# Attention step of a pipelined decoder: TensorE's groups in a new order, with ScalarE and VectorE following

## What is computed

```python
xn = layernorm(x)
q, k, v = xn @ Wq, src @ Wk, src @ Wv          # src is xn, or ctx in a cross attention
s = einsum('bhqd,bhkd->bhqk', q, k) * scale (+ mask or relative positions)
o = softmax(s) @ v
x = x + o @ Wo (+ bo)                          # L1_xattn, L3_xattn: a layer norm after it
```

## Time and profile before

| what | value |
|---|---|
| profiled execution | 4900.09 us, its span 4898.2 us |
| median of three runs | 4896.48 us |
| TensorE busy | 4007.7 us, 82% of the span |
| VectorE, GpSimd busy | 65%, 61% |
| mean granted TensorE clock | 0.889 |
| DMA | mean 28 GB/s |

### The profile page before, as it was taken

One profiled execution on the slowest core, in us unless ns is written; L12 is line 12 of the kernel. 1 busy time (PEld: TensorE's weight loads), 2 busy tenths in 40 slices (PEclk: granted clock), 3 DMA queues, 4 the chain that ended last, 5 costly groups with the idle time before them and its releaser, 6 DMA issues. The chain is left out here.

```text
span 4898.2 us, 215645 instructions
## 1 busy us (share of the span) xinstructions
PE 4007.7 (82%) x85067; PEld 2918.6 (60%) x85076; DVE 3203.4 (65%) x10848; ACT 2059.5 (42%) x5737; POOL 2994.6 (61%) x4949
## 2 busy tenths in 40 slices
PE   8999977254899978656999997559879998889988
PEld 6777754132566666523777774335547776667766
DVE  5875668422344688787556874753337878888866
ACT  4555545011344444365555554112225543336632
POOL 6766632276455699688556762038876777777710
PEclk9999988555899998755999997879998999999999
DMA  3000012433100022200000002113431000000000
GB/s 94 5 13 19 19 28 57 78 62 54 37 0 0 18 39 39 35 1 1 2 0 15 22 18 54 42 46 75 77 62 35 0 15 16 16 9 1 0 13 24
DMA packets 380509, 139.58 MB, mean 28 GB/s; under 512 B 216487, under 2 KB 373239, under 8 KB 380055
## 3 DMA queue, kind: packets, MB, share of 16 engines
q1 hardware_dynamic: 345430, 107.60, 9.3%
q0 software_dynamic: 34816, 28.34, 4.0%
HBM read 91.46 MB, written 43.85 MB: 28 GB/s over the span
## 5 line engine op out<-in xcount | busy, mean ns | idle before, releaser
L1051 DVE TENSOR_REDUCE rowmax<-ps 128x16 f32<-128x1024 f32 x512 | 626.3, 1223 | 488.0 <-PE ps L678 487.7
L696 PE MATMUL ps<-prob,kT 32*64 32x256 f32 x9216 | 781.7, 408 | 8.7 <-issue 2.4
L721 PE MATMUL ps<-v,probT 64*64 64x64 f32 x36864 | 764.6, 227 | 5.3 <-issue 2.2
L721 PEld LDWEIGHTS ps<-v,probT 64*64 64x64 f32 x36864 | 683.8, 140 | 57.4 <-issue 16.0
L678 PE MATMUL ps<-kblock,qT 32*64 32x256 f32 x8192 | 697.0, 410 | 17.2 <-DVE rowmax L1060 14.2
L900 ACT ACTIVATE probT<-ps 128x1024 f32<-128x1024 f32 x512 | 518.0, 1012 | 353.4 <-PE ps L708 353.0
L585 POOL TENSOR_TENSOR kblock<-kT,key_scale 128x512 f32<-128x512 f32 x576 | 599.8, 1041 | 18.2 <-ACT kT L878 7.6
L587 POOL TENSOR_TENSOR prob<-qT,key_scale 128x512 f32<-128x512 f32 x576 | 601.5, 1044 | 0.0
L561 POOL TENSOR_TENSOR vareps<-moments,eps 128x1 f32<-128x1 f32 x522 | 98.8, 189 | 745.7 <-DVE negmean L1025 745.6
L887 ACT ACTIVATE xn<-x_res,nmr,rstd 128x128 f32 (+1 forms) x512 | 252.7, 494 | 513.6 <-POOL nmr L567 349.5
L708 PEld LDWEIGHTS ps<-mT,pick_bf 32*64 32x64 bf16 x16384 | 311.7, 108 | 221.2 <-ACT mT L857 74.1
(11 more groups left out here) (380 smaller groups left out, 9655.7 us busy)
## 6 DMA issues: line engine op xcount, KB each, us to landing
ctxT<-in_ctxT SPq DMA_DIRECT2D x256, 64.0 KB, 1.8
held<-in_g_w SPq DMA_DIRECT2D x16, 836.0 KB
ctxT<-in_ctxT SPq DMA_DIRECT2D x256, 32.0 KB, 1.9
table<-prob SPq DMA_DIRECT2D x32, 256.0 KB, 2.4
x_dram<-x_res SPq DMA_DIRECT2D x32, 256.0 KB, 2.4
x_res<-x_dram SPq DMA_DIRECT2D x16, 512.0 KB, 6.9
x_res<-in_x SPq DMA_DIRECT2D x8, 512.0 KB, 7.5
x_res<-in_e_w SPq DMA_DIRECT2D x64, 64.0 KB
```

Source lines behind the costliest of these rows:

```text
L696: mm = nc.tensor.matmul(out.rearrange("p (h s) -> p h s", h=GH), k.kT[rows, buf, S * b:S * b + S], k.qblock[rows, buf, :, S * b:S * b + S] ...
L721: mm = nc.tensor.matmul(k.ps_o[S * b:S * b + S, u, S * hh:S * hh + S], k.probT[rows, buf, at:at + S], k.v9[rows, buf, (HD + 1) * h:(HD + 1 ...
L1051: nc.vector.tensor_reduce(spread, heads, AX.X, ALU.max).then_inc(soft.did["max_raw"], 1)
```

## The change

TensorE's step becomes: front, then out, values and turn, then scores, then mixing. The waits move too: everything that the scores wait for (`max_done` of it-4, `kblock_done` of it-3, the exponential of it-6, `qblock_done` of it-5) and what the mixing waits for (`exp_done`) now stands ahead of the output projection; before, it stood ahead of the scores or of the transpose of the maxima. ScalarE copies the front group's results first and oT and v after them. VectorE takes the maxima first and normalises the mixed values last. GpSimd's order stays.

```diff
@@ attention_pe, step
         mm = None
+        if mixes is not None:
+            after(pe, c, "v_done", it, mb)
+        after(pe, c, "kT_done", it, 3)
...
+            nc.tensor.matmul(k.ps_q, weights(project, 0), k.xnT[:, b2, 0:P], start=True, stop=True)
...
+            mm = nc.tensor.transpose(k.ps_xT, k.xn[:, b1, :], k.ident)
+        if less is not None:
+            after(pe, c, "max_done", it, 5)
+            mm = nc.tensor.matmul(k.ps_mT, top_halves(k.rowmax[:, b5, :]), k.ident_bf[:, :], start=True, stop=True)
+        if mm is not None:
+            mm.then_inc(c.front_psum, 1)
+
+        mm = None
+        if score1 is not None:
+            after(pe, c, "max_done", it, 4)
+            after(pe, c, "kblock_done", it, 3)
+        if score2 is not None:
+            after(pe, c, scores_read(c, it, 6), it, 6)
+            after(pe, c, "qblock_done", it, 5)
+        if mixes is not None:
+            after(pe, c, "exp_done", it, mb)
         if value is not None or turn is not None or out is not None:
             after(pe, c, values_read(c, it, 4), it, 4)
             after(pe, c, "y_read", it, 9)
             after(pe, c, "oT_done", it, 8)
         if out is not None:
             mm = nc.tensor.matmul(k.ps_y, k.oT[:, b8, :], weights(out, 3), start=True, stop=True)
+        if mixes is not None and turn is None:
+            after(pe, c, "on_done", it, mb + 1)
...
-        if mixes is not None:
-            for hh in range(HEADS // 2):
-                mm = mix(mixes, (par - mb) % NB, hh)
-            mm.then_inc(mixes.did["o_psum"], 1)
-        if not early:
-            scores_writable(score1, score2, it)
         for bk in range(2):
...
             mm.then_inc(score2.did["s2_psum"], 1)
+
+        if mixes is not None:
+            for hh in range(HEADS // 2):
+                mm = mix(mixes, (par - mb) % NB, hh)
+            mm.then_inc(mixes.did["o_psum"], 1)
@@ attention_act, step
-        if turn is not None:
...
-        if value is not None and value.name not in VALUE_BIAS:
...
         if norm is not None or project is not None or soft is not None:
             act.wait_ge(c.front_psum, c.fronts(it))
...
+        if turn is not None:
...
+            nc.scalar.activation(k.oT[:, b7, :], k.ps_oT, ACT.Copy).then_inc(turn.did["oT_done"], 1)
+        if value is not None and value.name not in VALUE_BIAS:
...
@@ attention_dve, step
-        mixes, mb = c.mixing(it)
-        if mixes is not None and mixes.softmax:
...
         if soft is not None:
             after(dve, c, "s1_psum", it, 3)
...
+        mixes, mb = c.mixing(it)
+        if mixes is not None and mixes.softmax:
+            inv = k.rowinv[:, :].rearrange("p (u h e) -> p u h e", u=2, e=1)
...
```

More of the change, by code:

```diff
@@ L725, in mix @@
         return mm
-    def values_mixable(mixes, it, mb):
-        if mixes is not None:
[L729 to L739, removed]
     def step(it, par):
@@ L751, in step @@
         mm = None
+        if mixes is not None:
+            after(pe, c, "v_done", it, mb)
+        after(pe, c, "kT_done", it, 3)
+        if c.steady is None:
+            after(pe, c, "xT_done", it, 2)
+            after(pe, c, "mT_done", it, 6)
+        if project is not None:
+            if project.cross:
+                after(pe, c, "ctx_loaded", it, 2, each=32)
+            nc.tensor.matmul(k.ps_q, weights(project, 0), k.xnT[:, b2, 0:P], start=True, stop=True)
+            mm = nc.tensor.matmul(k.ps_k, weights(project, 1),
+                                  k.ctxT[:, b2, 0:P] if project.cross else k.xnT[:, b2, 0:P], start=True, stop=True)
+        if norm is not None:
+            after(pe, c, "xn_done", it, 1)
+            mm = nc.tensor.transpose(k.ps_xT, k.xn[:, b1, :], k.ident)
[13 more added lines that the diff above has]
+            after(pe, c, "exp_done", it, mb)
         if value is not None or turn is not None or out is not None:
@@ L878, in step @@
                 nc.scalar.activation(k.kT[:, b2, :], k.ps_k, ACT.Copy).then_inc(project.did["kT_done"], 1)
+        if turn is not None:
+            act.wait_ge(c.yv_psum, it - 2)
+            after(act, c, "y_read", it, 8)
+            if c.name(it, 3) in VALUE_BIAS:
+                after(act, c, values_read(c, it, 3), it, 3)
+            nc.scalar.activation(k.oT[:, b7, :], k.ps_oT, ACT.Copy).then_inc(turn.did["oT_done"], 1)
+        if value is not None and value.name not in VALUE_BIAS:
+            act.wait_ge(c.yv_psum, it - 2)
+            after(act, c, "y_read", it, 8)
+            after(act, c, "o_psum", it, 3 + NB)
+            nc.scalar.activation(values(k, b3), heads_of(k.ps_v), ACT.Copy).then_inc(value.did["v_done"], 1)
         if plain is not None:
```

36 lines of the change are left out of this document (13 added, 23 removed).

## The result

The changed kernel takes 5142.98 us (median of four runs, 5138.79 to 5150.06) against 4897.55 us (four runs) before: a ratio of 1.0505, 95% interval 1.0486 to 1.0523. It is 5% slower; the forecast was 5142, +246. The profiled execution took 5140.97 us, its span is 5139.1.

The account below looks back on a forecast made before the run. TensorE (4.43 us a step) and an equally long VectorE-GpSimd circle were taken to bound L0_attn, the latter L3_ffn. Over 60 steps a stage, +106 +61 +27 +28 -15 +39 = +246 on 4896 gave 5142 us, range 4955 to 5250.

Parts of the forecast that it names:

- The circle: One output projection to the next, through VectorE, GpSimd and held subtractions: 1.05 + 2.00 + 2.07 + 0.30 = 5.42 us in L0_attn.
- 2.00: Microseconds from VectorE's stream update to GpSimd's L585, through the moments and the norm's small operations.
- 2.07: Microseconds from the start of GpSimd's L585 to the end of the maxima, with both subtractions held.
- The 0.30 behind `max_done`: TensorE passing seven waits between the maxima's end and the output projection: 0.30 us, between 0.05 and 0.45.
- the case of 5.86: L2_attn: first subtraction just behind L587's start, second then behind L611, 0.44 us more; the middle, 5.64, was taken.
- The two cases weighed there: L3_ffn: first subtraction ahead of L585, step about 5.0 us, or L585 first, 6.02; 5.5 was taken.
- the case of 5.0: L3_ffn: first subtraction ahead of L585, so only L585 holds the second; step about 5.0 us.
- TensorE's own 4.43: TensorE's work in a step of L0_attn, 4.43 us without a gap worth naming, taken to stay after the change.
- rival 1: The hold doesn't form and stages fall to what TensorE needs: -95, so 4800 us; chance 0.14.
- the hold: VectorE's subtractions with both inputs in SBUF wait until the running GpSimd operation ends; forecast to delay TensorE 0.7 us a step.
- Rival 2: First subtraction waits for L585, but second slips ahead of L587, or the signal costs nothing: 4980 us; chance 0.14.
- Rivals 3 and 4: 3: TensorE bounds before and after, 4896 us, chance 0.04; 4: idle TensorE gets a lower clock, 5240 us, chance 0.08.

Follow-up runs that it names:

- a1: Changed kernel without the two VectorE subtractions that end the row maxima (L1_xattn keeps them): 5080.62 us, ratio 1.0372.
- a5: Changed kernel with two small one-input VectorE operations in place of the two subtractions (L1_xattn keeps its own): 5080.19 us, ratio 1.0372.
- d2: Changed kernel with all its computation, ScalarE's exponential put ahead of its normalization: 5129.93 us, ratio 1.0478.
- a2: Kernel before the change, without the two subtractions (L1_xattn keeps them): 4786.61 us, ratio 0.9773.
- d1: Changed kernel without the two subtractions (L1_xattn keeps them) and with ScalarE's exponential ahead of its normalization: 4944.27 us, ratio 1.0091.
- f1: Changed kernel without the two subtractions, exponential ahead of normalization, four satisfied waits moved from the output projection to the projections: 4888.68 us, ratio 0.9988.
- b2: Changed kernel with VectorE's order of before, reciprocal and normalized values ahead of the maxima: 5828.34 us, ratio 1.1896.

## Why the prediction was right, step by step

- **The circle.** Right in kind and in place: L1031 asks inside L585, L1034 ends with L587, L773 waits for it. a1 and a5 show that the two-input subtractions make it, d2 that in L0_attn they make it alone. Of its terms 2.00 measured 2.01 and 2.07 measured 2.07. The 1.05 from the output projection to the stream update measured 1.14 in the step shown and up to 1.22 in the others; L785 ends at 227.40, so that is 0.15 of signal and start where I had put 0.05.
- **The 0.30 behind `max_done`.** Wrong: 0.06 in three steps of four, 0.22 in the fourth. I took the gap of the earlier trace rows as a price of the count of waits (scaled by seven to four its 0.28 is 0.49, and not the 0.45 that I put as the bound). What counts is how much stands behind the wait that comes last, and the maxima are the last in the compiled list in three steps of four. The error is masked by the 0.09 to 0.17 above: three steps of four measure 5.28 to 5.35, the fourth 5.53, together 5.38 against 5.42.
- **L0_xattn, L3_attn.** 5.55 and 5.57 against 5.62, for the same reason.
- **L2_attn.** 5.55 against 5.64. The first subtraction does come just behind L587's start (2503.76 against 2503.71) and is held for 1.02, but the second then takes 0.17, for no L611 follows; the case of 5.86 doesn't exist there.

```profile
2503.76 1.02 DVE L1031 TENSOR_TENSOR rowmax<-rowmax 128x16 f32<-128x16 f32 x1
2504.82 0.17 DVE L1034 TENSOR_TENSOR rowmax<-rowmax 128x16 f32<-128x16 f32 x1
```

- **L1_attn.** 6.34 against 6.25, a gain of 0.17 instead of 0.25 a step.
- **L3_ffn.** 5.82 against 5.5. The two cases weighed there both occur: L585 is first in about every fourth step, L1031 in the three others. GpSimd's L585, L1031 and L1034, and L773 that follows, first for the one and then for the other:

```profile
4754.53 1.04 POOL L585 TENSOR_TENSOR kblock<-kT,key_scale 128x512 f32<-128x512 f32 x1
4754.55 1.05 DVE L1031 TENSOR_TENSOR rowmax<-rowmax 128x16 f32<-128x16 f32 x1
4755.63 0.96 DVE L1034 TENSOR_TENSOR rowmax<-rowmax 128x16 f32<-128x16 f32 x1
4756.65 0.30 PEld L773 LDWEIGHTS ps<-attn_w,oT 128*128 128x128 f32 x2 [1.25 <-DVE rowmax L1034]
...
4760.34 0.17 DVE L1031 TENSOR_TENSOR rowmax<-rowmax 128x16 f32<-128x16 f32 x1
4760.42 1.04 POOL L585 TENSOR_TENSOR kblock<-kT,key_scale 128x512 f32<-128x512 f32 x1
4760.55 0.94 DVE L1034 TENSOR_TENSOR rowmax<-rowmax 128x16 f32<-128x16 f32 x1
4761.00 1.00 ACT L890 ACTIVATE probT<-ps 128x1024 f32<-128x1024 f32 x1
4762.44 0.30 PEld L773 LDWEIGHTS ps<-attn_w,oT 128*128 128x128 f32 x2 [1.13 <-DVE rowmax L1034]
```

  Where L1031 comes 0.08 ahead of L585 it takes 0.17, and the maxima are done at 4761.49, a microsecond before the next L773. The rule cited from the Trainium skill (SBUF — State Buffer, Who interferes with whom), that whoever starts first has the shared ports, fits VectorE's side of this; that GpSimd is then blocked no row shows, as L585 takes its 1.04 there too. That is the case of 5.0. But the exponential ends at 4762.00, and with 0.44 more the step is as long as the other. The step that failed is the sum for this stage, which had no ScalarE in it: a1, without the subtractions, stays at 5.78, and d2, with the exponential first, gives 5.21. (The trace names L1034 as the releaser of the last row, though it had ended 0.95 before; the two runs say that it was ScalarE.)
- **L1_xattn.** Zero was forecast, +0.25 measured, inside the bounds given (-0.2 to +0.4). Its transposes were 5.7 to 6.3 apart and are now 4.0 to 9.1, while GpSimd's busy share falls from 93% to 265.68/298.79 = 89%. TensorE waits 52.8 us in these 48 steps for VectorE's normalized values, of the mixing that now comes last, and the granted clock is 0.85 instead of 0.90:

```profile
1875.98 0.41 PE L779 MATMUL ps<-attn_w,ctxT 128*128 128x64 f32 x2 [1.80 <-DVE o L1059]
```

  That this wait is the cause is argued from the trace; no run took it away.
- **TensorE's own 4.43.** Wrong in both directions and without effect on the sum: 4.33 to 4.36 in the old order once the subtractions are gone (a2; in the kernel before the product L794 starts 1.49 after the output projection in the median, in a2 1.39, so a wait of 0.1 on the maxima was in the 4.43), 4.62 to 4.64 and every fourth step 4.89 in the new one (d1). It hits rival 1: had the hold not formed, the exponential's circle (5.21) would have stood in its place, and the time would have been the 5081 of a1, not 4800. That rival's price left out ScalarE, and with it the prediction gave 0.14 to a gain that couldn't come.
- **With the hold or without it.** Without the subtractions in either kernel the new order still costs 5081 against 4787 (a1, a2): 294 us, more than the 245 of the change itself. So the hold is what bounds the plain stages of the changed kernel, but not what the change's loss needs: with it away the exponential's circle, the waits passed and what f1 leaves open take its place. The prediction had the first circle right and did not see the others.
- **Rival 2.** Its second case came true in part, as the signal costs 0.06, but not its step of 4.8 to 5.0, which its own terms don't give either (5.12 + 0.05). Its first case is out: in L0_attn L1034 is held in every step.
- **Rivals 3 and 4.** The hold is no longer beside TensorE's work but ahead of it, so 3 is out; 4 needs a lower clock, and the clock stayed at 1.00 in the plain stages. b2 shows it where TensorE idles longer.

The sum by measured steps times 60 is 3 x 0.88 (0.82, 0.84 and 0.97 in the plain stages), 2 x 0.39, -0.17, +0.97, +0.25 and +0.01: 4.47 x 60 = 268 us, against 250 measured over the chains and 246 forecast. The counts of 60 are a little high, L3_ffn and L1_xattn were taken too low and the rest slightly too high; that the forecast hits within 1 us is partly luck.

## What to carry to other kernels

When a wait is moved ahead of the group from which its own releaser is fed, a side path becomes a circle: add up every engine's chain from one start of that group to the next, and price each rival with all of them, ScalarE too.
